# A gated convolution block with a top-8 expert layer: x and out stored in 4-KB runs, LayerNorm statistics of two tiles at a time, and one load of the last stage moved to ScalarE's queue

## What is computed

```
x: (1, 384, 384, 128)                       # 147456 tokens of 128 channels, fp32
xn   = LN(LN(x)) * norm_a + norm_b          # over the 128 channels
left = (xn@Wl + bl) * sigmoid(xn@Wlg + blg);  right = (xn@Wr + br) * sigmoid(xn@Wrg + brg)
gate = sigmoid(xn@Wog + bog)
mix  = einsum('bkjd,bkid->bijd', left, right) / 384          # one 384x384x384 product per channel
x    = x + (LN(mix)*on_a + on_b) * gate @ Wo + bo
t    = LN(x);  probs = softmax over the tokens of t@gate_w.T + gate_b   # 64 experts
top 8 tokens of each expert are pooled by their weights, go through the expert's
two-layer net (gelu), and the result is added to those 512 rows of t
out  = t + that
```

## Time and profile before

| | |
|---|---|
| median of 3 runs | 3180.3 us (3177.96 to 3189.99) |
| profiled execution | 3181.94 us, its span 3180.1 us |
| stage 1 | some 0 to 1180 us |
| stage 2 and what ends it | some 1180 to 1915 us |
| stage 3 | some 1915 to 3060 us |
| tail | the last 120 us |
| busiest engines over the span | DVE 85%, PE 84%, ACT 75%, POOL 60% |

### The profile page before, as it was taken

How to read it: one execution, slowest core, us unless ns; L and a number is a source line. 1 busy time by engine, 2 the same in 40 slices (tenths; PEclk the granted TensorE clock), 3 DMA queues, 4 the chain that set the end, 5 groups by cost and what they waited for, 6 DMA issues and landing times.

```text
span 3180.1 us, 69636 instructions
## 1 busy us (share of the span) xinstructions
PE 2664.8 (84%) x15070; PEld 2139.5 (67%) x15070; DVE 2707.8 (85%) x8274; ACT 2375.4 (75%) x4284; POOL 1899.8 (60%) x2343
## 2 busy tenths in 40 slices
PE   7999999999999989989999956767767767676745
PEld 5777777777777778888888854555555545455523
DVE  7999999999999979999999996878778778787872
ACT  6888888888888877888888855877777777776740
POOL 8888888888888860000000006877778778787842
PEclk9999999999999999999999987999999999999977
DMA  5777777777777768999999967999999998998946
GB/s 192 260 258 258 260 262 259 263 260 258 258 259 264 259 253 318 332 322 332 340 335 329 335 232 247 275 293 283 282 289 289 290 295 269 287 285 278 282 141 196
DMA packets 668228, 873.01 MB, mean 275 GB/s; under 512 B 29223, under 2 KB 523970, under 8 KB 668194
## 3 DMA queue, kind: packets, MB, share of 16 engines
q1 hardware_dynamic: 659394, 855.31, 79.3%
q10 hardware_dynamic: 8448, 16.78, 1.5%
q0 software_dynamic: 352, 0.53, 0.2%
HBM read 492.97 MB, written 379.52 MB: 274 GB/s over the span
## 4 chain that ended last, share of the span: by engine, by line
PE 53%; DMA 27%; DVE 6%; issue 6%; ACT 4%; SPq 2%; POOL 1%; ACTq 0%; DVEq 0%; POOLq 0%
PE banks L1254 33%; DMA statrow<-stat_d 15%; DMA arena<-left_d 11%; PE banks L1322 9%; PE banks L1243 4%; PE banks L1313 3%; PE banks L1323 2%; ACT arena L792 2%; ACT work L862 1%; PE banks L1288 1%; PE banks L1340 1%; PE banks L1332 1%; DVE arena L1001 1%; DVE bn L1070 1%; SPq L470 1%
## 5 line engine op out<-in xcount | busy, mean ns | idle before, releaser
L1254 PE MATMUL banks<-x_parts,w_parts 128*128 128x512 f32 x4320 | 1104.6, 404 | 0.8 <-POOL x_parts L609 0.8
L1254 PEld LDWEIGHTS banks<-x_parts,w_parts 128*128 128x128 f32 x4320 | 770.5, 189 | 220.6 <-DVE arena L944 83.8
L1288 PE MATMUL banks<-left_parts,right_parts 128*128 128x384 f32 x3456 | 630.9, 340 | 60.7 <-ACT arena L793 50.2
L1288 PEld LDWEIGHTS banks<-left_parts,right_parts 128*128 128x128 f32 x3456 | 602.8, 190 | 88.9 <-issue 85.3
L862 ACT ACTIVATE work<-arena,nmr,rs 128x128 f32<-128x128 f32 x1152 | 458.9, 481 | 215.1 <-POOL nmr L678 206.0
L642 POOL COPY rcol<-late 128x8 f32 (+1 forms) x144 | 28.7, 199 | 717.3 <-ACT late L808 717.3
L647 POOL TENSOR_TENSOR arena<-arena,work 128x512 f32<-128x512 f32 x288 | 360.7, 1274 | 158.2 <-DVE arena L1050 157.9
L1322 PE MATMUL banks<-wo_sb,arena 128*128 128x128 f32 x2304 | 422.4, 314 | 0.1
L944 DVE SCALAR_TENSOR_TENSOR arena<-banks,cols,arena 128x512 f32<-128x512 f32 x576 | 404.6, 742 | 18.1 <-ACT arena L758 7.5
L1322 PEld LDWEIGHTS banks<-wo_sb,arena 128*128 128x128 f32 x2304 | 383.2, 205 | 32.5 <-issue 3.2
L609 POOL TENSOR_TENSOR x_parts<-xn,x_parts 128x512 fp32r<-128x512 f32 x288 | 374.2, 1300 | 4.6 <-ACT x_parts L746 4.6
(11 more groups left out here) (173 smaller groups left out, 4534.2 us busy)
## 6 DMA issues: line engine op xcount, KB each, us to landing
arena<-in_x_dram SPq DMA_DIRECT2D x144, 512.0 KB, 3.7
left_d<-arena SPq DMA_DIRECT2D x144, 512.0 KB, 2.6
right_d<-arena SPq DMA_DIRECT2D x144, 512.0 KB, 3.4
gate_d<-arena SPq DMA_DIRECT2D x144, 512.0 KB, 4.2
arena<-right_d SPq DMA_DIRECT2D x128, 576.0 KB, 5.8
arena<-left_d SPq DMA_DIRECT2D x128, 576.0 KB, 6.8
mixed_d<-arena SPq DMA_DIRECT2D x128, 576.0 KB, 4.3
work<-mixed_d SPq DMA_DIRECT2D x144, 512.0 KB, 4.3
```

The lines of the kernel that those rows point to most:

```text
L1254: last = nc.tensor.matmul(ps[2 + k][:, :], w_parts[:, wq, k], x_parts[:, xq, b, c], start=((wq, xq) == TERMS[0]), stop=((wq, xq) == TERMS[ ...
L1288: last = nc.tensor.matmul(ps[NT * b + t][:, 0:GRID], lr_parts[RIGHT][:, rq, b, k, t * P:(t + 1) * P], lr_parts[LEFT][:, lq, b, k], start=( ...
```

## The change

Three things are changed.

1. x comes into the launch, and out leaves it, as an array of (step, partition, tile, channel). A partition's eight tiles of a step are then one run of 4 KB where they were eight runs of 512 bytes. The row that an indirect DMA has to name for a token is worked out from the token's number by shifts and masks in the tail.
2. The statistics of two tiles are taken by one `bn_stats`, whose input walks the two tiles in turn (a channel of the one, the same channel of the other), so that its even and its odd half are the two tiles. The eight instructions become four over twice the elements, and the `bn_aggr` that joined two halves are gone in stages 1 and 3. The mean is read from where `bn_stats` wrote it, and the variance is its sum of squares times 1/128, a factor that the small operation behind it takes in.
3. The load of `statrow` in stage 3 is issued by ACT, behind the scaling of step s, and no longer by SP. The two of the first steps stay with SP.

```diff
-            def load_parts(i, b):
-                s = 2 * i + b
-                sp.wait_ge(s_z3, mark(2, s - 2, 2))
-                settle(sp, s_tick_sp)
-                sp.dma_start(statrow[0:KR, b], stat_r[s].broadcast_to([PARTS, 2 * PARTS, 2 * CHUNK])).then_inc(s_sin[b], 16)
+            def first_parts(b):
+                sp.dma_start(statrow[0:KR, b], stat_r[b].broadcast_to([PARTS, 2 * PARTS, 2 * CHUNK])).then_inc(s_sin[b], 16)
...
-                sp.dma_start(out_step[s], late_arena[:, 1, b].rearrange("p h (c d) -> p (h c) d", c=TILES)).then_inc(s_ost[b], 16)
+                sp.dma_start(out[s], late_arena[:, 1, b].rearrange("p h (c d) -> p (h c) d", c=TILES)).then_inc(s_ost[b], 16)
...
-                    if in_range(i, b, 2, STEPS):
-                        load_parts(*shifted(i, b, 2))
...
+            def load_parts(i, b):
+                s = 2 * i + b
+                act.wait_ge(s_z3, mark(2, s - 2, 2))
+                act.dma_start(statrow[0:KR, b], stat_r[s].broadcast_to([PARTS, 2 * PARTS, 2 * CHUNK])).then_inc(s_sin[b], 16)
+
...
                     if in_range(i, b, 0, STEPS):
                         scale_rest(i, b)
+                    if in_range(i, b, 2, STEPS):
+                        load_parts(*shifted(i, b, 2))
                     if in_range(i, b, -1, STEPS):
                         normalise(*shifted(i, b, -1))
...
                 dve.wait_ge(s_xin[b], 16 * (i + 1))
-                for t in range(2 * TILES):
-                    last = nc.vector.bn_stats(bn[:, b, t], xin[:, b, t])
+                dve.wait_ge(s_xhp, mark(1, s - 2, 1))
+                settle(dve, s_tick_dve)
+                for q in range(TILES):
+                    last = nc.vector.bn_stats(six(bn[:, b, q]), two_tiles(xin[:, b, 2 * q:2 * q + 2]))
                 last.then_inc(s_bn, 1)
                 dve.wait_ge(s_bn, mark(1, s, 1))
-                dve.wait_ge(s_xhp, mark(1, s - 2, 1))
-                settle(dve, s_tick_dve)
-                for t in range(2 * TILES):
-                    last = nc.vector.bn_aggr(mv[:, b, t], bn[:, b, t])
-                last.then_inc(s_ag, 1)
-                dve.wait_ge(s_ag, mark(1, s, 1))
-                nc.vector.tensor_scalar(vv[:, b], mv[:, b, :, 1], 1.0 + EPS, EPS_CONV_IN * EPS,
+                nc.vector.tensor_scalar(over_tiles(vv[:, b]), bn[:, b, :, :, SQUARES], (1.0 + EPS) / DIM, EPS_CONV_IN * EPS,
                                         ALU.mult, ALU.add).then_inc(s_var, 1)
...
-            nc.vector.tensor_copy(rowidx[:, :], rowpick[:, 0, :]).then_inc(s_ri, 1)
+            link(nc.vector.tensor_copy(token[:, :], rowpick[:, 0, :]))
+            nc.vector.tensor_scalar(rowpart[:, 0], token[:, :], STEP_BITS, STEP_BITS, ALU.logical_shift_right, ALU.logical_shift_left)
+            nc.vector.tensor_scalar(rowpart[:, 1], token[:, :], P - 1, TILE_BITS, ALU.bitwise_and, ALU.logical_shift_left)
+            link(nc.vector.tensor_scalar(rowpart[:, 2], token[:, :], P_BITS, 2 * TILES - 1, ALU.logical_shift_right, ALU.bitwise_and))
+            link(nc.vector.tensor_tensor(rowpart[:, 0], rowpart[:, 0], rowpart[:, 1], ALU.bitwise_or))
+            nc.vector.tensor_tensor(rowidx[:, :], rowpart[:, 0], rowpart[:, 2], ALU.bitwise_or).then_inc(s_ri, 1)
```

More of the change, by code:

```diff
@@ L16 @@
+import math
 from contextlib import ExitStack
@@ L37 @@
 PARTS = 3
+P_BITS = 7
+TILE_BITS = 3
+STEP_BITS = P_BITS + TILE_BITS
 EPS_CONV_IN = 1e-6
@@ L100, in build @@
     KR = 2 * PARTS * PARTS
-    x_tok = x.rearrange("b i j d -> (b i j) d")
-    out_tok = out.rearrange("b i j d -> (b i j) d")
+    out_rows = out.rearrange("s p t d -> (s p t) d")
     left_d = nc.dram_tensor("left_d", (DIM, TOKENS), FP32, kind="Internal").ap()
@@ L213, in build, with mean_of, over_tiles, two_tiles @@
         rowsign = sb("rowsign", [2 * PARTS, 2])
-        bn = sb("bn", [P, 2, 2 * TILES, 6])
-        mv = sb("mv", [P, 2, 2 * TILES, 2])
+        bn = sb("bn", [P, 2, TILES, 2, 3])
+        mv = sb("mv", [P, GROUPS, 2])
+        MEAN, SQUARES = 1, 2
+        def mean_of(b, t):
+            return bn[:, b, t // 2, t % 2, MEAN:MEAN + 1]
+        def over_tiles(v):
+            return v.rearrange("p (q t) -> p q t", t=2)
+        def two_tiles(v):
+            return v.rearrange("p t d -> p d t")
+        def six(v):
+            return v.rearrange("p t k -> p (t k)")
         vv = sb("vv", [P, 2, 2 * TILES])
@@ L1068, in statistics3, with moments3 @@
                 dve.wait_ge(summed_by, mark(1, 2 * i + b, 1))
-                for c in range(TILES):
-                    last = nc.vector.bn_stats(bn[:, b, TILES * h + c], summed[:, b, h, c])
+                for q in range(TILES // 2):
+                    last = nc.vector.bn_stats(six(bn[:, b, TILES // 2 * h + q]), two_tiles(summed[:, b, h, 2 * q:2 * q + 2]))
                 if h:
                     last.then_inc(s_bn, 1)
-            def aggregate3(i, b):
+            def moments3(i, b):
                 s = 2 * i + b
@@ L1078, in aggregate3 @@
                 settle(dve, s_tick_dve)
-                for t in range(2 * TILES):
-                    last = nc.vector.bn_aggr(mv[:, b, t], bn[:, b, t])
-                last.then_inc(s_ag, 1)
-            def moments3(i, b):
-                s = 2 * i + b
-                dve.wait_ge(s_ag, mark(1, STEPS + s, 1))
-                nc.vector.tensor_scalar(minus[:, b], mv[:, b, :, 0], -1.0, None, ALU.mult)
-                nc.vector.tensor_scalar(vv[:, b], mv[:, b, :, 1], 1.0, EPS, ALU.mult, ALU.add).then_inc(s_v3, 1)
+                nc.vector.tensor_scalar(over_tiles(minus[:, b]), bn[:, b, :, :, MEAN], -1.0, None, ALU.mult)
+                nc.vector.tensor_scalar(over_tiles(vv[:, b]), bn[:, b, :, :, SQUARES], 1.0 / DIM, EPS,
+                                        ALU.mult, ALU.add).then_inc(s_v3, 1)
             def best_values(i, b):
@@ L1416 @@
     r = run_bass_kernel_spmd(nc, [arrays], core_ids=[0])
-    return r.results[0]["out_0_dram"]
+    return by_token(r.results[0]["out_0_dram"], np.shape(inputs["x"]))
```

51 lines of the change are left out of this document (29 added, 22 removed).

## The result

The changed kernel is slower: 3221.9 us median (3214.6 to 3235.1, four runs) against 3181.6 of the kernel before (3178.0 to 3190.0, four runs, the same chip). The ratio is 1.0115, 95% interval 1.0083 to 1.0147. The forecast of 3141 was wrong, on the other side of no change and outside its range.

A forecast was written before the change was run, and what follows sets the result against it. Stage 1 was taken as bound by DVE's cycle, stage 3 by the ring over statrow's load. Stage 1 +20, stage 3 -60 and tail +0.8 gave -39, so 3141 us on the median's scale, range 3048 to 3202.

The forecast's parts named there:

- the rings of 6.98 and 7.05: Stage 3: DVE's own loop, 6.98 us a step, and a chain over two steps, 14.09/2 = 7.05, after the change.
- DVE's round: Stage 1: DVE's cycle of statistics, `vv`, `rs`, centring and products sets the period, 8.07 us a step.
- I take a cycle more per element: Strided `bn_stats` on DVE: 1.04 ns more per element, four take 2.45 us, 0.14 lost a step, stage 1 +20 us.
- the rival of reads at full speed: Strided DVE reads at full or nearly full speed: whole kernel 3047 us, or 3065 at 0.66 ns; chance 0.28.
- 7.76: Stage 1: PE's own period in us a step, taken as half between 7.45 and 8.07; PE bounds if reads are cheap.
- the prediction's own signs of being wrong: `bn_stats` off, ACT's sequencer reaching the load late, or weights on its queue starving `statrow` for much longer than 10 us.
- on its own queue they don't wait for those: Stage 3: `statrow`'s packets on ACT's queue no longer stand behind the store and load of x issued some 3 us before.
- 3.58: Stage 3: us from `statrow`'s landing through `outer` and projection to the next issue; the period is landing + 3.58.
- 0, give or take 2 us each, 14 in all: Stage 3: change in `statrow`'s delay at the seven weight loads, counted as 10 us both before and after.
- the queue brings nothing: Rival: `statrow`'s landing stays 4.0 us, stage 3 stays 7.57 a step, stage 1 pays 20; 3201 us, chance 0.10.
- the 3.3: Stage 3: `statrow`'s landing time in us after the change, from 4.0, including whatever the runs of 4 KB give.
- three rivals: Reads at full or nearly full speed (0.28), the queue brings nothing (0.10), and dear strided reads, 3216 us (0.12).

The follow-up runs named there:

- e9: Changed kernel with statrow's load back on SP and the seven weight loads moved behind stage 3, loop still in eight pieces; 0.9592 of the kernel before.
- e7: Kernel before with only the interleaved statistics, statrow on SP and runs of 512 bytes kept; 0.9807 of the kernel before.
- e3: Changed kernel in which SP issues mix and gate only after ACT has issued statrow of the step before; 0.9933 of the kernel before.
- e1: Changed kernel with only statrow's load put back on SP's queue in its old place; 3081 us, 0.9673 of the kernel before.
- e8: Kernel before with only the runs of 4 KB for x and out, statrow on SP; 0.9908 of the kernel before.
- e10: e3 with the seven weight loads moved behind stage 3, loop still cut into eight pieces; 0.9782 of the kernel before.
- e4: e1 with mix and gate issued one place earlier, ahead of statrow, all on SP's queue; 1.0595 of the kernel before.
- e12: e1 with the weights in 14 loads of 1 MB in place of 7 of 2 MB; 0.9807 of the kernel before.

## Why the prediction was wrong

**The reading of before held.** Stage 3 is a ring of the issue of `statrow`, its landing, `outer` and the projection. That the three parts of the table add up to the period is so by the way they are taken; what bears the ring out is that the period moved with each part that an experiment moved. In e9, at 7.04, other waits are longer than the one for `statrow`, as the rings of 6.98 and 7.05 said. That DVE's round sets stage 1 also held, but only for the first 0.27 us: the round lost 1.5 us of work, 1.07 in the statistics and 0.44 in the centring, and the period fell from 8.06 to 7.79.

**Part 1, wrong in sign, by its size.** The step that failed is "I take a cycle more per element". It took the stride of ACT's exponential for DVE's. Measured is 1.44 for the four, not 2.45, so the rival of reads at full speed was right. 7.76 was its period, and 7.79 came, -39 us in stage 1 in place of +20; that it came so near is in part luck, since 7.76 was the middle of a span from 7.45 to 8.07 with no row for it. The rule in the Trainium skill (Advanced Engine Details and Errata, section Memory Cachelines) forecast a penalty here. By this trace it doesn't hold for DVE's `bn_stats` with neighbouring reads 512 bytes apart. In stage 3 the statistics gave 8 us (20 by the median, e7), for the ring over `statrow` binds there.

**Part 2, the step that decided it.** The failed sentence is: "Off SP's queue the load also no longer holds back the loads of mix and gate by its wait; these had landed early anyway, as no wait names them." It asked only whether mix and gate gain by coming earlier. They don't; what they do is to come ahead of `statrow`. SP's wait had been the thing that kept 1 MB out of its way. Restoring the order alone (e3) brings the kernel from 1.0115 to 0.993, from slower than before to faster. But the order is only some two fifths of what the move costs, 45 of 125 us in stage 3 or 58 of 141 by the ratios. The rest came with ACT's queue even in the right order (e3 over e1, 80 us), by the weights in it, the later issue and the lower clock. Two of the prediction's own signs of being wrong point there, that ACT's sequencer reaches the load late and that the weights starve it: it was 0.13 us later a step, and the steps with weights took 15.2 to 17.3 us in place of 11.5 to 14.6. Then "on its own queue they don't wait for those": issue to `outer` was to fall from 4.0 to 3.3, and is 3.85 after 3.91, and against e1, with the same layout, it rose from 3.56. And "3.58", the rest of the ring, was held fixed. It is 3.69 before and 4.13 after, by the issue 0.13 later and by a projection at the lower clock behind longer idle times of PE. Without the eight longest steps the ring is 0.38 longer, 51 us of the 73.

The weights were counted "0, give or take 2 us each, 14 in all". The eight longest steps together take 122.7 us against 103.1, +20. With what follows a long step, the weights on ACT's queue account for 42 us between e3 and e1 by the profiles, and for 22 by the ratios.

The Trainium skill's rule (DMA: Bandwidth & Descriptors, section "Issuing engines are not separate DMA queues") was cited and given one chance in ten. By it the landing stays, and that part came out so. Its rival, "the queue brings nothing", left stage 3 at 7.57 a step, though. It didn't have the loss, since it too left the order of issue out.

**Part 3** was put into the 3.3 and nothing else. By e8 it is worth 0.9%: issue to `outer` 0.21 shorter, and 31 us in stage 3. The landing of x in stage 1 went from 3.7 to 3.4, hidden as forecast.

**Part 4** held: +0.8 forecast, +0.73 measured.

**The sum.** Forecast: stage 1 +20, stage 3 -60, tail +1. Came: -39, +73, +1. With the right price of the reads and the queue left alone it would have been -39 and -52 (e1). The forecast and its three rivals shared one assumption: that a load moved to another queue can at worst bring nothing.

## What to carry to other kernels

A wait in a queue is also an order for everything behind it. Before a transfer is moved to another engine, list what stood behind its wait, and ask how many bytes may now be issued ahead of it in the time of one landing. In these runs a small load that a ring waits for was better kept on the queue of the bulk transfers, ahead of them, than on another engine's queue, which carried rare big loads as well (e1 against e3), and also with those gone (e9 against e10). Where a ring contains matmuls, a longer wait can be paid twice, by itself and by the clock of the matmuls behind it. It was where PE stood idle meanwhile, as in the changed kernel; in e9, where PE had other work, it was not (last item below).

## What the runs showed of the hardware

- DVE's `bn_stats` over 256 elements in the order of two tiles, neighbours 512 bytes apart, takes 424 ns in the mean against 271 for 128 in a row. Per element there is no difference that the stride would explain.
- DVE's centring of 128 elements takes 431 to 433 ns with its mean in the array that `bn_stats` wrote, and 521 with the mean in `mv`. POOL's doesn't change. Why was not tried.
- A load of 36 KB on ACT's queue, issued 0.8 us behind 1 MB on SP's, is there no sooner than one on SP's queue in the same order: 4.22 us from issue to `outer` in the mean of 32 steps, 4.00 in e4. The landing of this load itself is not in the traces' figures.
- A load of 1 MB of weights lengthens the step it falls in by 3.2 us (e12, mean of 14), one of 2 MB by 4.5 (e1, mean of 7).
- Behind an issue-to-outer time over 3.9 us the projection takes 3.18 in the changed kernel and 3.66 in e4, behind one under 3.3 it takes 2.55 and 2.60 (steps of over 11 us and those just ahead of them left out). In e9 the two are 2.63 and 2.59. PE had been idle before the `outer` of the long ones for 2.18 us in the mean in the changed kernel, 3.23 in e4 and 0.96 in e9. In the one such step whose windows are shown the granted clock is 0.57.
